# Cross attention with two-bank maxima, one-bank exponentials and maxima parts on GpSimd

## What is computed

```python
q = (x @ Wq + bq)          # 4 x 256 queries, 16 heads of 16 channels
k, v = ctx @ Wk + bk, ctx @ Wv + bv     # 4 x 4096 keys
s = q @ k.T / sqrt(16)     # per batch and head: 256 x 4096, masked keys at -inf
p = softmax(s)
x = x + (p @ v) @ Wo + bo
```

## Time and profile before

| what | value |
|---|---|
| median of 3 runs | 2339.08 us (2335.96 to 2340.39) |
| the profiled execution, its own time | 2341.5 us |
| its span (first to last instruction) | 2339.6 us |
| busy: PE, DVE, ACT, POOL | 1977.5, 1446.2, 1023.7, 280.2 us |
| the two passes, ahead of the loop | 1107 to 1157 us |
| the loop with both passes | 1157 to 1754 us |
| the loop with the second pass only | 1754 to 1795 us |

### The profile page before, as it was taken

One profiled execution on the slowest core, in us unless ns is written; L12 is line 12 of the kernel. 1 busy time (PEld: TensorE's weight loads), 2 busy tenths in 40 slices (PEclk: granted clock), 3 DMA queues, 4 the chain that ended last, 5 costly groups with the idle time before them and its releaser, 6 DMA issues.

```text
span 2339.6 us, 37126 instructions
## 1 busy us (share of the span) xinstructions
PE 1977.5 (85%) x14824; PEld 1034.5 (44%) x14824; DVE 1446.2 (62%) x2697; ACT 1023.7 (44%) x1248; POOL 280.2 (12%) x137
## 2 busy tenths in 40 slices
PE   7989758888699999994999999999998468956867
PEld 5666535545466667672122223232323233532443
DVE  2223243530575675655999999999992665235566
ACT  3221114666442342331187888787887005201510
POOL 2222034766000000002000000000000100020000
PEclk9989979999799999996599999999999769977978
DMA  7211014777411211203623334252300350036100
GB/s 267 72 42 49 1 46 128 227 227 227 136 37 37 73 36 36 72 1 55 119 50 68 80 57 91 50 98 50 69 21 6 47 62 20 19 54 73 34 5 18
DMA packets 109978, 167.38 MB, mean 72 GB/s; under 512 B 17495, under 2 KB 78057, under 8 KB 105581
## 3 DMA queue, kind: packets, MB, share of 16 engines
q1 hardware_dynamic: 109692, 165.06, 29.3%
q0 software_dynamic: 128, 0.13, 0.1%
HBM read 123.81 MB, written 41.03 MB: 70 GB/s over the span
## 4 chain that ended last, share of the span: by engine, by line
PE 46%; DVE 37%; SPq 6%; DMA 4%; issue 3%; ACT 3%; POOL 2%; DVEq 0%; ACTq 0%; POOLq 0%
DVE mx_part L1860 25%; PE bank L1025 9%; PE pair L1041 9%; SPq L662 4%; PE pair L1321 2%; DVE mx L1949 2%; PE bank L874 2%; PE bank L240 2%; PE bank L918 1%; PE bank L1225 1%; PE pair L1175 1%; PE bank L291 1%; PE pair L1275 1%; PE bank L1284 1%; PE bank L854 1%
## 5 line engine op out<-in xcount | busy, mean ns | idle before, releaser
L1860 DVE TENSOR_REDUCE mx_part<-bank 128x1 f32<-128x512 f32 x1024 | 616.8, 675 | 11.6 <-PE bank L1090 10.2
L1477 ACT ACTIVATE pexp<-pair 128x1024 f32<-128x1024 f32 x512 | 520.2, 1033 | 171.5 <-PE pair L1123 168.6
L1090 PE MATMUL bank<-kst,qs 49*128 49x512 f16 x1024 | 376.6, 405 | 23.0 <-DVE mx_part L1860 10.4
L1123 PE MATMUL pair<-qs,kst 52*128 52x256 f16 x2048 | 347.0, 276 | 0.0
L1109 PE MATMUL bank<-pexp,vst 128*17 128x256 f32 x4096 | 321.4, 386 | 5.7 <-ACT oT L1467 5.4
L1090 PEld LDWEIGHTS bank<-kst,qs 49*128 49x128 f16 x1024 | 95.4, 93 | 353.1 <-issue 198.4
L1436 ACT ACTIVATE hid_f<-bank,b 128x512 f32<-128x512 f32 x160 | 109.9, 687 | 257.4 <-PE bank L1025 257.4
L1041 PE MATMUL pair<-w_lo,hid_hi 128*128 128x256 f16 x640 | 174.5, 273 | 0.0
L1041 PE MATMUL pair<-w_hi,hid_lo 128*128 128x256 f16 x640 | 174.5, 273 | 0.0
L1041 PE MATMUL pair<-w_hi,hid_hi 128*128 128x256 f16 x640 | 174.5, 273 | 0.0
L1488 ACT ACTIVATE pexp<-pair 128x1024 f32<-128x1024 f32 x64 | 65.5, 1023 | 150.2 <-PE pair L1245 148.7
(11 more groups left out here) (270 smaller groups left out, 3276.3 us busy)
## 6 DMA issues: line engine op xcount, KB each, us to landing
kst<-k_scr SPq DMA_DIRECT2D x192, 128.0 KB
w_f<-in_w_all SPq DMA_DIRECT2D x20, 1024.0 KB, 7.3
v_scr<-v_st SPq DMA_DIRECT2D x64, 272.0 KB, 2.6
vst<-v_scr SPq DMA_DIRECT2D x16, 1088.0 KB, 5.2
ctx_sb<-in_ctx SPq DMA_DIRECT2D x16, 1024.0 KB, 4.9
cT<-in_ctxT SPq DMA_DIRECT2D x32, 512.0 KB, 4.6
k_scr<-k_hi SPq DMA_DIRECT2D x128, 64.0 KB, 2.6
k_scr<-k_lo SPq DMA_DIRECT2D x128, 64.0 KB, 2.3
```

The costliest lines, as they stand in the source:

```text
L1090: pe.matmul(bank[RING[n % 3]], qs[g % NBK][rws, p, qt * P:(qt + 1) * P], kst[g % NBK][rws, p, kb * 512:(kb + 1) * 512], start=True, stop=T ...
L1123: return pe.matmul(pair[c % 2][:, (2 * e + p) * S:(2 * e + p + 1) * S], kst[g % NBK][head_rows(e, X_MAX + 3), p, c * P:(c + 1) * P], qs[g ...
L1477: act.activation(pexp[n % NP_][:, :, :].rearrange("p h q -> p (h q)"), pair[c % 2][:, :], ACT.Exp, scale=SCALE).then_inc(s_exp, 1)
L1860: dve.tensor_reduce(mx_part[:, at:at + 1], bank[RING[n % 3]], X_AXIS, ALU.max).then_inc(s_mx, 1)
```

## The change

- First pass: two products (e = 0 and e = 1 of the same query tile and key block) are written side by side into a pair of banks, and one DVE reduction of 128x1024 with two results takes the place of two of 128x512. These PAIRS = 32 pairs in a group rotate over two pairs of banks, 4/5 and 6/7; a pair of products waits until the reduction of two pairs ago is done. One pair goes with each step, ahead of all the four scores.
- Second pass: the scores of each half e go to a single bank and are exponentiated by an operation of their own, 128x512, two in a step. The banks rotate over 0, 1 and 2 (`SCORE_BANKS`), so that the scores of unit n wait for the exponential of unit n-3. The result buffers become 8 halves of the same memory. `weigh` waits for each half separately and accumulates in bank 3.
- Maxima: the final maximum of a group goes to `mx_grp` (128x8). GpSimd negates and splits it with five small operations, each of which waits for the one before. Two steps after step 23 (TURN_LAG) DVE turns the 128x32 parts with its own 32x32 transpose, and SP stores them with 8 DMAs in place of 6. The PE transpose of the maxima and the five DVE operations are gone.
- Some semaphores of the last router are shared with those of the first one; the order of that work stays as it is.

```diff
@@ -440,8 +441,15 @@
...
         NP_ = 4
-        pexp = [sb(f"pexp{i}", [P, GH, S], F32, attention_scope) for i in range(NP_)]
-        mx_part = sb("mx_part", [P, GH * 2 * (S2 // 512)], F32, attention_scope)
+        pexp_all = sb("pexp_all", [P, NP_ * GH * S], F32, attention_scope)
+        pexp = [pexp_all[:, GH * S * i:GH * S * (i + 1)].rearrange("p (h q) -> p h q", h=GH) for i in range(NP_)]
+        unit_exp = [pexp_all[:, 2 * S * i:2 * S * (i + 1)] for i in range(NUE)]
+        mx_part = sb("mx_part", [P, 2, 4, S2 // 512], F32, attention_scope)
+        mx_grp = sb("mx_grp", [P, 2, GH], F32, attention_scope)
+        neg_grp = sb("neg_grp", [P, 2, GH], F32, attention_scope)
+        res_grp = sb("res_grp", [P, 2, GH], F32, attention_scope)
+        prt_grp = sb("prt_grp", [P, 32], F16, attention_scope)
+        prt_rows = sb("prt_rows", [P, 32], F16, attention_scope)
         mx = sb("mx", [P, 128], F32, attention_scope)
...
@@ -580,26 +584,27 @@
...
         EXP_BLOCKS = (8, 16)
-        S1N = GH * 2 * (S2 // 512)
+        PAIRS = GH * (S2 // 512)
         COPY_STEP = 2
         NORM_STEP = 4
+        TURN_LAG = 2
+        MROW = 16 * 2 * (P // 32)
         MAX_STEP = 23
-        PER_STEP = S1N // CH
-        AHEAD = PER_STEP * (CH - 1 - MAX_STEP)
-
-        RING = (0, 1, 3)
+        AHEAD = CH - 1 - MAX_STEP
 
...
             if c <= MAX_STEP:
-                return [(g + 1, AHEAD + PER_STEP * c + i) for i in range(PER_STEP if g + 1 < NG else 0)]
-            return [(g + 2, PER_STEP * (c - 1 - MAX_STEP) + i) for i in range(PER_STEP if g + 2 < NG else 0)]
+                return [(g + 1, AHEAD + c)] if g + 1 < NG else []
+            return [(g + 2, c - 1 - MAX_STEP)] if g + 2 < NG else []
 
...
 
-            f, p, qt, kb, e = i // 32, i // 16 % 2, i // 8 % 2, i // 2 % 4, i % 2
-            return p, e, qt, 4 * f + kb
+            f, p, qt, kb = i // 16, i // 8 % 2, i // 4 % 2, i % 4
+            return p, qt, 4 * f + kb
+
+        SCORE_BANKS = (0, 1, 2)
 
...
@@ -730,10 +735,11 @@
...
             def max_rows(g):
-                for i in range(3):
-                    for e in range(2):
-                        at = HALF * e + X_MAX + i
-                        sp.dma_start(qs[g % NBK][at:at + 1, :, :], m_prt[4 * e:4 * e + 4, i, :]).then_inc(s_mrow, 16)
+                for e in range(2):
+                    at = HALF * e + X_MAX
+                    for b in range(P // 32):
+                        dst = qs[g % NBK][at:at + 3, :, :].rearrange("i p (t b n) -> i (p t) b n", t=2, n=32)[:, :, b, :]
+                        sp.dma_start(dst, prt_rows[32 * b + 12 * e:32 * b + 12 * e + 12, :]).then_inc(s_mrow, 16)
 
...
@@ -1078,80 +1084,69 @@
...
 
-                p, e, qt, kb = product_of(i)
+                p, qt, kb = product_of(i)
                 if i == 0:
                     pe.wait_ge(s_q[g % NBK], 96 * (g // NBK + 1))
-                if i % (S1N // 2) == 0:
-                    pe.wait_ge(s_kh[g % NBK][i // (S1N // 2)], 128 * (g // NBK + 1))
+                if i % (PAIRS // 2) == 0:
+                    pe.wait_ge(s_kh[g % NBK][i // (PAIRS // 2)], 128 * (g // NBK + 1))
                 n = ring.next()
-                if n >= 3:
-                    pe.wait_ge(s_mx, n - 2)
-                rws = head_rows(e, X_MAX)
-                pe.matmul(bank[RING[n % 3]], qs[g % NBK][rws, p, qt * P:(qt + 1) * P],
-                          kst[g % NBK][rws, p, kb * 512:(kb + 1) * 512], start=True, stop=True).then_inc(s_s1, 1)
-
-            def turn_maxima(g):
-                pe.wait_ge(s_mxa, g + 1)
-                n = ring.next()
-                pe.wait_ge(s_mx, n - 2)
-                pe.transpose(bank[RING[n % 3]][0:2 * GH, 0:P], mx[:, 0:2 * GH], ident[:, :]).then_inc(s_s1, 1)
+                if n >= 2:
+                    pe.wait_ge(s_mx, n - 1)
+                for e in range(2):
+                    rws = head_rows(e, X_MAX)
+                    last = pe.matmul(pair[n % 2][:, e * 512:(e + 1) * 512], qs[g % NBK][rws, p, qt * P:(qt + 1) * P],
+                                     kst[g % NBK][rws, p, kb * 512:(kb + 1) * 512], start=True, stop=True)
+                last.then_inc(s_s1, 1)
 
             def weigh(g, c):
-                pe.wait_ge(s_exp, g * CH + (c + 1))
                 if c == 0:
...
                         pe.wait_ge(s_oc, g)
-                slot = (g * CH + c) % NP_
-                for p in range(2):
-                    for e in range(2):
+                for e in range(2):
+                    n = 2 * (g * CH + c) + e
+                    pe.wait_ge(s_exp, n + 1)
+                    for p in range(2):
                         h = 2 * p + e
-                        last = pe.matmul(bank[2][32 * h:32 * h + HV, 0:S], vst[g % 2][:, c, h * HV:(h + 1) * HV],
-                                         pexp[slot][:, 2 * e + p, :], start=(c == 0), stop=(c == CH - 1))
+                        last = pe.matmul(bank[3][32 * h:32 * h + HV, 0:S], vst[g % 2][:, c, h * HV:(h + 1) * HV],
+                                         unit_exp[n % NUE][:, p * S:(p + 1) * S], start=(c == 0), stop=(c == CH - 1))
                 last.then_inc(s_pv, 1)
...
                 n = ring.next()
-                pe.wait_ge(s_mx, n - 2)
+                pe.wait_ge(s_mx, n - 1)
                 for qt in range(2):
-                    last = pe.transpose(bank[RING[n % 3]][:, qt * P:(qt + 1) * P], oT[g % 2][:, qt * P:(qt + 1) * P],
-                                        ident[:, :])
+                    last = pe.transpose(pair[n % 2][:, qt * P:(qt + 1) * P], oT[g % 2][:, qt * P:(qt + 1) * P], ident[:, :])
                 last.then_inc(s_s1, 1)
             def scores(g, c, e, p):
-                return pe.matmul(pair[c % 2][:, (2 * e + p) * S:(2 * e + p + 1) * S],
+                n = 2 * (g * CH + c) + e
+                return pe.matmul(bank[SCORE_BANKS[n % 3]][:, p * S:(p + 1) * S],
                                  kst[g % NBK][head_rows(e, X_MAX + 3), p, c * P:(c + 1) * P],
...
 
-            for i in range(S1N):
+            for i in range(PAIRS):
                 first_pass(0, i)
-            turn_maxima(0)
             for i in range(AHEAD):
...
 
-                pe.wait_ge(s_mrow, g * 96 + 96)
+                pe.wait_ge(s_mrow, MROW * (g + 1))
                 for c in range(CH):
-                    beside = first_pass_at(g, c)
-                    if g * CH + c >= 2:
-                        pe.wait_ge(s_exp, g * CH + (c - 1))
-                    if beside:
-                        first_pass(*beside[0])
-                        scores(g, c, 1, 0)
-                        scores(g, c, 1, 1)
-                        first_pass(*beside[1])
-                        scores(g, c, 0, 0)
-                        scores(g, c, 0, 1).then_inc(s_s2, 1)
-                    else:
-                        scores(g, c, 0, 0)
-                        scores(g, c, 1, 0)
-                        scores(g, c, 0, 1)
-                        scores(g, c, 1, 1).then_inc(s_s2, 1)
+                    for other, i in first_pass_at(g, c):
+                        first_pass(other, i)
+                    n = 2 * (g * CH + c)
+                    if n >= 3:
+                        pe.wait_ge(s_exp, n - 2)
+                    scores(g, c, 0, 0)
+                    if n >= 2:
+                        pe.wait_ge(s_exp, n - 1)
+                    scores(g, c, 1, 0)
+                    scores(g, c, 0, 1).then_inc(s_s2, 1)
+                    scores(g, c, 1, 1).then_inc(s_s2, 1)
                     if c == NORM_STEP - 1 and g >= 1:
                         turn_out(g - 1)
-                    if c == MAX_STEP + 1 and g + 1 < NG:
-                        turn_maxima(g + 1)
                     if c >= 2:
...
@@ -1464,18 +1459,18 @@
...
                 act.wait_ge(s_pv, g * CH + CH)
-                act.activation(oT[g % 2][:, :], bank[2][:, 0:S], ACT.Copy).then_inc(s_oc, 1)
+                act.activation(oT[g % 2][:, :], bank[3][:, 0:S], ACT.Copy).then_inc(s_oc, 1)
 
...
                         copy_out(g - 1)
-                    n = g * CH + c
-                    act.wait_ge(s_s2, n + 1)
-                    if n >= NP_:
-                        act.wait_ge(s_pv, n - NP_ + 1)
-                    act.activation(pexp[n % NP_][:, :, :].rearrange("p h q -> p (h q)"), pair[c % 2][:, :], ACT.Exp,
-                                   scale=SCALE).then_inc(s_exp, 1)
+                    for e in range(2):
+                        n = 2 * (g * CH + c) + e
+                        act.wait_ge(s_s2, n + 1)
+                        if n >= NUE and e == 0:
+                            act.wait_ge(s_pv, (n - NUE) // 2 + 1)
+                        act.activation(unit_exp[n % NUE], bank[SCORE_BANKS[n % 3]], ACT.Exp, scale=SCALE).then_inc(s_exp, 1)
             copy_out(NG - 1)
...
@@ -1855,9 +1850,9 @@
...
                     dve.wait_ge(s_mxa, g)
-                p, e, qt, kb = product_of(i)
```

(107 more changed lines are left out.)

## The result

The changed kernel takes 2315.1 us (median of 5 runs, 2314.1 to 2327.2) against 2339.1 before: a ratio of 0.9886, with a 95% interval of 0.9857 to 0.9915. Run again with other experiments it gave 0.9883 (0.9858 to 0.9908). It is 24 us faster. The forecast was 2304 us, 35 us less than before. The measured time lies in the range of 2292 to 2332, but the saving is a third smaller than forecast, and one step of the forecast, the way of the maxima to the next group, is wrong.

What follows compares the result with a forecast made beforehand. DVE was taken as the bound, PE 0.055 us a step behind. Terms: -36.4 us in the loop with both passes, -3.2 ahead, +4.5 with one pass, -35.1 from 2339.1: 2304 us, 8-in-10 range 2292 to 2332.

Steps and rivals of the forecast that it cites:

- the way of the maxima to the next group: From PE's start of step 23: maxima rows in at 9.7 to 10.5 us, next group starting at 10.35, just fitting.
- a stall of 0.1: At each group's start: 0.1 us waiting for maxima rows, inside 0.4 us added for pauses; 0 to 0.6 in the range.
- DVE bounds, PE right behind: Loop with both passes: DVE's step falls from 1.195 to about 1.137 us, PE's is 1.15, so the two are tied.
- The exponentials: Second pass on ACT: 0.60 us for each 128x512 exponential, two at 1.0 to 1.10 us, below PE's 1.15 us step.
- The issues: Maxima rows on SP's queue: 8 DMAs at 0.617 us each, the last starting 4.3 us after the first.
- The transpose: DVE reaches its transpose of the maxima after the reductions of steps 24 and 25, 3.8 us after PE's start of step 23.
- The landing: Last DMA of a group's maxima rows: lands 1.3 to 2.1 us after its issue starts.
- GpSimd: Five dependent maxima operations, 0.25 to 0.5 us each, 1.2 to 2.4 in all: hidden, or holding DVE up to 0.5 us.
- Ahead of the loop and behind it: Before the loop with both passes -3.2 us (bounds -2 and -4); loop with one pass +4.5 us (bounds +2 and +10).
- The rest of the program at 0: Everything outside the stage of the two passes keeps its order: 0 us change.

Runs made afterwards that it cites:

- MAX_STEP 21: Changed kernel with MAX_STEP 21 in place of 23, so the next group's maxima are complete two steps earlier: 2299.2 us, ratio 0.9806; again in more rounds 2296.2 us.
- the light DVE: Changed kernel with MAX_STEP 21, its reductions reading only 256 of the 512 columns of each bank: 2264.6 us, ratio 0.9664.
- the split: Changed kernel with four of the eight DMAs of the maxima rows issued from GpSimd, beside four from SP: 2295.9 us, ratio 0.9794.

## Why the forecast was right and where not

The time came out in the range, but in part by luck: two errors went opposite ways. The steps are quicker than forecast, a group without late rows takes 37.32 us and not 38.0, about -10 us in the loop. The late rows cost 1.2 us a group, where a stall of 0.1 was taken, about +18 us. Without them the time is below the forecast of 2304 us: 2299.2 and 2296.2 us are measured with MAX_STEP 21.

- **DVE bounds, PE right behind: right.** The pair of reductions was forecast at 1.137 us and runs at 1.131 ((36.29 - 1.216) / 31, from the row of 32 ahead of the loop). PE's order was taken at 1.15 and is 1.10 (the light DVE shows it). I had put PE's step (1.15) above DVE's (1.137); it is the other way round, by 0.03 us. The rows of one undisturbed step gave 1.14, too long by 0.04; the lower bound of 1.13 that I set was not low enough.
- **The exponentials: right.** 0.595 us each, 0.98 us for two back to back ((27.55 - 0.595) / 55 = 0.49 us each in the loop with one pass). The rule of the Trainium skill ("ScalarE: Activation LUTs", section "What ACT_TABLE_LOAD costs") gave an estimated 0.613 and 1.04; the measurement lies 3 to 6% below it. A bias operand makes ACT the bound, as the forecast said of longer exponentials.
- **The maxima's way to the next group: wrong.** The forecast had the rows in 9.7 to 10.5 us after PE's start of step 23, just in time, with 0.1 us of stall. They came after 12.1 us (1222.84 to 1234.92). Two terms were mis-sized. The issues: the forecast carried the old form over at 0.617 us and set the last issue 4.3 us after the first. The new form takes 5.97 us for eight, 0.746 us each, and its last issue began 5.3 us after the first: 1.0 us more. The transpose: it came at 4.8 us instead of 3.8. The forecast's own terms give 4.2, as two reductions of 1.137 us follow the maximum that ends at 1.9; it set them level with PE's steps 24 and 25, and left out that the maximum holds them up. The other 0.6 us come from DVE lagging behind PE: the last pair of the group was reduced 2.2 us after its product began, and not 1.55. I had taken PE for the bound, but with DVE as the bound the pairs wait for it. The stall is 1.3 us on PE and 1.2 us in the period of each group. What was forecast as just fitting, with at most 0.6 us of stall, was late by 1.3.
- **The landing: right.** The last issue began at 1227.90 + 5.97 - 0.70 = 1233.17, and PE started at 1234.92, 1.75 us later, between my 1.3 and 2.1. The Trainium skill's "DMA: Bandwidth & Descriptors", section "Anatomy of one DMA — SWDGE (gpsimd) path", has about 2.0 us for DMAs from GpSimd. That is 0.25 us more than these from SP took; the four from GpSimd in the split landed 1.6 us after their issue, in the median, so the figure is too long here.
- **GpSimd: right, at the cheap end.** Five operations take 1.31 us for the 1.2 to 2.4 forecast.
- **Ahead of the loop and behind it: right.** -2.7 for -3.2; +4.4 for +4.5, though made up otherwise: the late rows cost 2.0 us there in place of 0.8, the exponentials 40 x (0.98 - 0.92) = 2.4 in place of 3.7.
- **The rest of the program at 0: not settled.** The profiles have it 3 to 9 us longer, the granted clock in it mostly lower, and the cause is open.

Together: -28.3 - 2.7 + 4.4 = -26.6 us in the stage of this profile (-24.3 in the second one), and -24 by the medians of whole runs.

## What to carry to other kernels

When the bound gets faster, ask for each result that has a due time how much it had to spare: here 2.6 us of slack turned into a wait, because two more and longer issues stood in one queue, the steps before the due time got shorter, and the bounding engine works behind the one that needs the result. Setting the work that produces it two steps earlier, one number, was worth 18 us, three quarters of what the change itself gave. And time a DMA's issue by its own form: one with four source rows of 256 bytes took 0.617 us of the queue, one with twelve of 64 bytes 0.746, for fewer bytes in all. Which feature of the form costs the time was not tried. And a total that comes out near the forecast is no proof of its terms: here a wait of 18 us and steps that were 10 us quicker stood against each other.

## What the runs showed of the hardware

GpSimd operations on 128x8 took 0.19 to 0.23 us each and 0.27 us with the semaphore wait between, less than the 0.46 us that a line through its large operations gave. Merging two reductions of 512 columns into one of 1024 from two PSUM banks saved 0.064 us of 1.195; consecutive ones overlapped by 0.08 us in either form (0.675 - 0.5975, and 1.216 - 1.131). Two exponentials on one bank each cost 0.98 us where one over two banks costs 0.92. The DVE transpose of 128x32 took 0.20 us. The granted clock fell to 0.50 for 3.4 us behind four of the six waits of 1.67 to 1.79 us for the maxima rows (the two profiles of the changed kernel and the one with GpSimd's part doubled), and behind none of the waits of 1.3 us in the loop with both passes.
